# Attention block with a gated feed-forward layer on one core: batch 0's output projection and second norm in the last fourteen steps of the attention loop instead of its middle

## The chip, the cores and the metric

One Trainium2 chip, one of its cores, one launch. The metric is the device time of the whole kernel in microseconds (us), lower is better. The engines are TensorE (PE in the profile; PEld its weight loads), VectorE (DVE), ScalarE (ACT), GpSimd (POOL) and SyncE (SP, which here only issues DMAs). Each runs its own instructions in the order in which they are written, and they meet only in semaphores.

## The reference

For x of shape (2, 1024, 256), in float32:

```python
x = x + quaternion_layer(x)                  # one 256x256 product
h = tc_rmsnorm_1(x, cond)                    # g * x * rsqrt(mean(x*x) + eps) + b, g and b from cond
q, k, v = h @ Wq.T, h @ Wk.T, h @ Wv.T       # 16 heads of 16
o = softmax(q k.T / 4) @ v
x = x + o @ Wo.T
y = tc_rmsnorm_2(x, cond)
x = x + (silu(y @ gate_w.T) * (y @ hid_w.T)) @ out_w.T     # hidden size 1024
```

## The kernel before

Tokens are 16 tiles of 128, in four chunks of 512: chunks 0 and 1 are batch 0, chunks 2 and 3 batch 1. There are three stages. A **preparation** makes q, k and v. The **attention loop** has 128 steps (`NSTEP`): for each of 8 groups of 4 heads (four groups a batch) and each half of 512 queries, eight steps over the tiles of 128 keys. What stands **behind the loop** (the list `fin`) is the feed-forward layer, 32 units of which (`("F", n)`) make gate and hidden products and then the output product, and between its first units the rest of the attention's output work.

In a **narrow step** (0 to 113) TensorE computes four score tiles of 512 columns for the softmax (L1214), four for the row maxima of a later group (L1141, reduced by VectorE, L982), and the products with v (L1249); ScalarE takes the exponentials (L850). From step `WIDE` = 114 on there are no maxima left: in these fourteen **wide steps** TensorE issues four score matmuls (L1230), then what else is placed there, then the four products with v of the step before (L1249, 512 columns), and ScalarE takes two exponentials of 1024 columns (L843). VectorE has almost nothing to do there. PSUM has eight banks: in the wide steps six of them hold three pairs of score tiles, bank 7 the products with v, and bank 6 is the only one for everything else.

**Side items** are put among the steps. ("T", n) transposes row maxima, ("O", n) the attention output of eight steps; they come every eighth step. The other items, in the table `placed`, are the work that follows the attention:

- ("a_T", c, k): four transposes (L1097) of attention output of chunk c, then its split in a high and a low part (`at_hi`, `at_lo`);
- ("WO", c, pair): the output projection of two token tiles, twelve matmuls of 256 columns (L1123), to which x is added;
- then the squares of the new x, their mean (`ms`), its inverse root by a power on GpSimd (L587), the scaled tokens `xs2`, and `add_residuals` on GpSimd (`x1 += attn`, 1024 columns, L592);
- ("y_T", c, k): four transposes of `xs2`, then the norm's scale and shift into `yn_f` and the split into `yn_hi` and `yn_lo`, which the feed-forward units of chunk c read.

For batch 0 these items stand at steps 60 to 90 before the change, and ScalarE empties their PSUM banks (a copy, or the norm's scale and shift) while GpSimd makes the two parts, adds x and scales the tokens. For batch 1 they stand behind the loop, where ScalarE, VectorE and GpSimd share them. An item in the loop holds its bank until its reader has counted a semaphore (`e_used`). The order on each engine is the order of the code; nothing is scheduled.

Of the kernel before, what the change touches and what calls it, by code (L numbers as in the profile page):

```python
# [22 lines left out]
P = 128  # L23
BATCH, SEQ, D = 2, 1024, 256
# [6 lines left out]
CT = 4  # L31
# [33 lines left out]
def build(nc, xt, cond, coef, wt, gwt, ft, out):  # L65
# [4 lines left out]
    with ctx:  # L70
# [109 lines left out]
        def head_rows(e, n):  # L180
# [14 lines left out]
        square_steps = {half_done + 1: (0, 0), half_done + 4: (0, 1), half_done + 12: (1, 0), half_done + 15: (1, 1)}  # L195
        mean_steps = {half_done + 6: 0, half_done + 17: 1}


        cuts = [placed[step] for step in sorted(placed) if placed[step][0] != "WO"]
        cut_no = {item: i for i, item in enumerate(cuts)}  # L200

# [23 lines left out]
        for step in range(NSTEP):  # L225
            for item in ([("S", step, i) for i in (2, 3) if step < WIDE] + side_items(step)
                         + [("S", step + 1, i) for i in range(2) if step + 1 < WIDE]):
                e_no[item] = len(e_no)
        wide_sides = {item for step in range(WIDE, NSTEP) for item in side_items(step)}
# [45 lines left out]
        for key, (n, _, _) in plan.items():  # L275
            if key[0] in ("QK", "V"):
# [5 lines left out]
        fin = ([("F", 0), last_output, ("a_T", 2, 0), ("a_T", 2, 1), ("F", 1), ("WO", 2, 0), ("WO", 2, 1), ("F", 2),  # L282
                ("a_T", 3, 0), ("a_T", 3, 1), ("SC", 2), ("F", 3), ("WO", 3, 0), ("WO", 3, 1), ("F", 4),
                ("y_T", 2, 0), ("y_T", 2, 1), ("F", 5), ("SC", 3), ("F", 6), ("y_T", 3, 0), ("y_T", 3, 1)]
               + [("F", n) for n in range(7, len(ffn_units) + OUT_LAG)])
# [57 lines left out]
        wo_added = sem("wo_added")  # L343
# [5 lines left out]
        cut_hi_ready = sem("cut_hi_ready")  # L349
        cut_ready = sem("cut_ready")  # L350
# [31 lines left out]
        def e_bank(*item):  # L382
            return psum[:, 6 if item in wide_sides else 4 + e_no[item] % EB, :]
# [32 lines left out]
        def wait_e_used(eng, *item):  # L416

            if item in (("T", 0), last_output):
                wait_evacuated(eng, *item)
            else:  # L420
                eng.wait_ge(e_used, e_no[item] + 1)
# [12 lines left out]

        def wait_cut(eng, *item):

            eng.wait_ge(cut_ready, cut_no[item] + 1)

        def cut_dst(item, part):
            hi_lo = (at_hi, at_lo) if item[0] == "a_T" else (yn_hi[item[1]], yn_lo[item[1]])  # L440
            return hi_lo[part][:, item[2], :]
# [116 lines left out]
        def _(pool):  # L558
# [35 lines left out]
            def low_part2(c, kt):  # L594
                pool.wait_ge(yn_hi_ready, KT * (c - BCH) + kt + 1)
                nc.gpsimd.tensor_tensor(yn_lo[c][:, kt, :], yn_f[:, kt, :], yn_hi[c][:, kt, :].bitcast(f32),
                                        ALU.subtract).then_inc(yn_lo_ready, 1)
# [41 lines left out]
            for step in range(NSTEP):  # L639
# [7 lines left out]
                for item in side_items(step):  # L647
                    if item[0] == "O":
                        normalise(item[1])
                    elif item[0] == "T":  # L650
                        split_maxima(item[1])
                    elif item[0] == "WO":
                        wait_e_used(pool, *item)
                        t = item[1] * CT + 2 * item[2]
                        nc.gpsimd.tensor_tensor(attn[:, t:t + 2, :], attn[:, t:t + 2, :], x1[:, t:t + 2, :], ALU.add
                                                ).then_inc(wo_added, 1)
                if step in mean_steps:
                    c = mean_steps[step]
                    pool.wait_ge(squares_done, NT + CT * (c + 1))
                    nc.gpsimd.tensor_scalar(ms[:, 1, c * CT:(c + 1) * CT], sumsq[:, 1, c * CT:(c + 1) * CT],  # L660
                                            1.0 / D, NEPS, ALU.mult, ALU.add).then_inc(ms_ready, 1)
                    inverse_root(1, c)
                    pool.wait_ge(inv_ready, NCH + c + 1)
                    t = slice(c * CT, (c + 1) * CT)

                    if c:
                        wait_e_used(pool, "y_T", c - 1, 1)
                    nc.gpsimd.tensor_tensor(xs2[:, :, :], attn[:, t, :],
                                            inv_rms[:, 1, t].unsqueeze(2).to_broadcast([P, CT, D]), ALU.mult
                                            ).then_inc(ys_ready, 1)  # L670
                    pool.wait_ge(ys_ready, c + 1)
                    add_residuals(c)
                    pool.wait_ge(x12_ready, c + 1)
                item = placed.get(step)
                if item in cut_no:
                    n = cut_no[item]
                    wait_e_used(pool, *item)
                    nc.gpsimd.tensor_copy(cut_dst(item, 0), yn_f[:, n % 2, :]).then_inc(cut_hi_ready, 1)
                    pool.wait_ge(cut_hi_ready, n + 1)
                    nc.gpsimd.tensor_tensor(cut_dst(item, 1), yn_f[:, n % 2, :], cut_dst(item, 0).bitcast(f32),  # L680
                                            ALU.subtract).then_inc(cut_ready, 1)
# [20 lines left out]
        def _(act):  # L702
# [16 lines left out]
            def norm_affine(norm, c, kt):  # L719
# [3 lines left out]
                if norm and c == BCH:  # L723
                    act.wait_ge(cut_ready, len(cuts))
                elif norm:
                    act.wait_ge(yn_lo_ready, KT * (c - BCH - 1) + kt + 1)
                elif c:
                    act.wait_ge(xn_lo_ready, KT * (c - 1) + kt + 1)
# [82 lines left out]
            def side_item(item):  # L811

                act.wait_ge(scores_filled, e_no[item] + 1)
                src = e_bank(*item)
                if item[0] == "T":
                    ins = copy_maxima(item[1], src)
                elif item[0] == "O":
                    ins = copy_outputs(item[1], src)
                elif item[0] == "WO":
                    t = item[1] * CT + 2 * item[2]  # L820
                    ins = nc.scalar.activation(attn[:, t:t + 2, :], src.rearrange("p (t d) -> p t d", t=2), ACT.Copy)
                else:
                    i = cut_no[item]
                    if i >= 2:
                        wait_cut(act, *cuts[i - 2])
                    if item[0] == "y_T":
                        ins = nc.scalar.activation(yn_f[:, i % 2, :], src, ACT.Identity,
                                                   scale=gb_col(item[1] // BCH, 1, 0, item[2]),
                                                   bias=gb_col(item[1] // BCH, 1, 1, item[2]))
                    else:  # L830
                        ins = nc.scalar.activation(yn_f[:, i % 2, :], src, ACT.Copy)
                ins.then_inc(e_used, 1)
# [3 lines left out]
            for s in range(NSTEP + 1):  # L836
# [15 lines left out]
                if s and s % LT == 0:  # L852
                    o = s // LT - 1
                    act.wait_ge(pv_done, s)
                    if o:
                        act.wait_ge(scores_filled, e_no["O", o - 1] + 1)
                    nc.scalar.activation(ot[:, :], O_BANK, ACT.Copy).then_inc(o_copied, 1)  # L857
                for item in side_items(s) if s < NSTEP else []:
                    side_item(item)

                if s in square_steps:
                    c, pair = square_steps[s]
                    act.wait_ge(wo_added, 2 * c + pair + 1)
                    for i in range(2):
                        sum_squares(1, c * CT + 2 * pair + i, attn[:, c * CT + 2 * pair + i, :])
# [41 lines left out]
        def _(dve):  # L907
# [76 lines left out]

            def reciprocal_sums(n):
# [52 lines left out]
            for s in range(NSTEP):  # L1038
# [4 lines left out]
                if s % LT == 2 and s > LT and len(max_items(s)) < 2:  # L1043
                    reciprocal_sums(s // LT - 1)

            for step in fin:
# [17 lines left out]
                if what == "SC":  # L1064
                    c = rest[0]
                    dve.wait_ge(squares_done, NT + CT * (c + 1))
                    mean_squares(1, c)
                    scale_tokens(1, c, attn, xs2, ys_ready)
# [24 lines left out]
        def _(pe):  # L1093
# [92 lines left out]
            def do_side(item):  # L1186

                what, n = item[0], item[1]
                pe.wait_ge(e_used, e_no[item] - (0 if item in wide_sides else EB - 1))
# [7 lines left out]
                elif what == "WO":  # L1197
                    wait_cut(pe, "a_T", n, 1)
# [4 lines left out]
                last.then_inc(scores_filled, 1)  # L1203
# [14 lines left out]
            def wide_scores(s, pair):  # L1218
# [3 lines left out]
                elif n == 2:  # L1222
                    pe.wait_ge(e_used, e_no["T", NG * NHALF - 1])
# [112 lines left out]
            pe.wait_ge(wide_used, wide_no(NSTEP, 0))  # L1336
            for step in fin:
# [24 lines left out]
                if n < len(ffn_units):  # L1362
                    c, ht = ffn_units[n]
                    if n == 0:
                        pe.wait_ge(cut_ready, len(cuts))
                        pe.wait_ge(fw_ready, len(fw_steps))
                    if ht == 0 and c >= BCH:
                        pe.wait_ge(yn_lo_ready, KT * (c - BCH + 1))
# [72 lines left out]
```

## Time and profile before

| what | value |
|---|---|
| time, median of 3 runs | 574.06 us (570.61 to 580.15) |
| the profiled execution's own time | 572.87 us |
| its span, first to last instruction | 571.1 us |
| mean granted TensorE clock | 0.991 of full |
| preparation ends, narrow steps begin | about 86 us |
| wide steps begin | about 394 us |
| loop ends, feed-forward begins | about 424 us |

The span is 1.8 us less than the time, which lies around it. Busy shares are averages over the three stages, which have different limits, so the stages are read one by one: the narrow steps in stretches of eight, the wide steps instruction by instruction.

### The profile page before, as it was taken

What the parts mean: (1) busy time and instruction counts of PE and PEld (TensorE: products, weight loads), DVE (VectorE), ACT (ScalarE), POOL (GpSimd) and SP (SyncE); (2) the same over time, 40 slices, a digit from 0 to 9 for tenths busy, and PEclk for the clock granted to TensorE, in tenths of its full rate; (3) what the DMA queues carried; (4) which work ended last, traced back from release to release, by engine and by line L of the source; (5) the groups of instructions that cost most, each with busy time, mean ns of one, the idle gap of its engine ahead of it and who ended that gap; (6) DMA issues with size and microseconds to landing.
All of it is one profiled execution on the core that took longest, in us unless ns stands there. A gap on an engine that the chain in (4) does not pass through costs nothing.

```text
span 571.1 us, 10548 instructions
## 1 busy us (share of the span) xinstructions
PE 550.7 (96%) x4272; PEld 308.6 (54%) x4272; DVE 381.6 (67%) x407; ACT 379.3 (66%) x734; POOL 157.6 (28%) x171
## 2 busy tenths in 40 slices
PE   8979999999999999999999999998999999999997
PEld 7765663333333333344343333333248988888886
DVE  5946878999999999988878989996004442121211
ACT  3643437888888888888879988988984432222322
POOL 5302430230231230031622620000005543233232
PEclk9997998999999999999999999999999999999999
DMA  5494984117017016006005100000000001010001
GB/s 215 148 310 166 248 254 137 34 40 146 7 41 151 1 50 104 1 3 114 2 5 92 22 5 1 3 3 3 1 1 1 1 0 39 1 37 1 27 12 38
DMA packets 15669, 35.21 MB, mean 62 GB/s; under 512 B 1900, under 2 KB 4588, under 8 KB 15620
## 3 DMA queue, kind: packets, MB, share of 16 engines
q1 hardware_dynamic: 13764, 27.98, 18.8%
q10 hardware_dynamic: 1856, 6.55, 4.0%
q8 instruction: 34, 0.56, 0.4%
q14 instruction: 15, 0.12, 0.1%
HBM read 19.48 MB, written 14.94 MB: 60 GB/s over the span
## 4 chain that ended last, share of the span: by engine, by line
PE 85%; ACT 6%; DVE 3%; issue 2%; DMA 2%; SPq 1%; POOL 0%; DVEq 0%; ACTq 0%
PE psum L1123 31%; PE psum L1141 26%; PE psum L1249 22%; PE psum L1097 3%; ACT prob L843 2%; ACT prob L850 2%; ACT ot L857 2%; DVE nmax L982 1%; DMA q_st<-scr_qk 1%; PE psum L1214 1%; PE psum L1230 1%; PE psum L1267 1%; PE psum L1173 1%; DMA qc<-in_coef 1%; DVE xs L971 0%
## 5 line engine op out<-in xcount | busy, mean ns | idle before, releaser
L982 DVE TENSOR_REDUCE nmax<-psum 128x1 f32<-128x1024 f32 x256 | 310.4, 1222 | 41.7 <-PE psum L1141 41.6
L850 ACT ACTIVATE prob<-psum 128x512 f32<-128x512 f32 x456 | 247.3, 597 | 37.1 <-PE psum L1214 18.5
L1141 PE MATMUL psum<-k_st,q_st 48*128 48x512 f32 x512 | 184.7, 451 | 5.1 <-DMA q_st<-scr_qk 4.5
L1214 PE MATMUL psum<-q_st,k_st 50*128 50x512 f32 x456 | 167.9, 447 | 0.5 <-ACT prob L850 0.3
L1249 PE MATMUL psum<-prob,v_sb 128*17 128x256 f32 (+1 forms) x1928 | 158.2, 400 | 6.4 <-ACT ot L857 4.3
L1141 PEld LDWEIGHTS psum<-k_st,q_st 48*128 48x128 f32 x512 | 75.9, 187 | 108.7 <-DVE nmax L982 60.9
L1081 DVE TENSOR_TENSOR h_f<-psum,silu_g 128x512 f32<-128x512 f32 x32 | 22.1, 691 | 101.0 <-PE psum L1123 94.5
L1249 PEld LDWEIGHTS psum<-prob,v_sb 128*17 128x17 f32 x1928 | 32.4, 95 | 85.6 <-ACT prob L850 61.5
L900 ACT ACTIVATE silu_g<-psum 128x512 f32<-128x512 f32 x32 | 19.1, 597 | 78.7 <-PE psum L1123 78.6
L1214 PEld LDWEIGHTS psum<-q_st,k_st 50*128 50x128 f32 x456 | 68.6, 185 | 3.7 <-ACT prob L850 2.3
L697 POOL TENSOR_TENSOR h_lo<-h_f,h_hi 128x512 fp32r<-128x512 f32 x32 | 41.6, 1299 | 71.0 <-ACT h_hi L876 71.0
L633 POOL TENSOR_TENSOR attn<-o_raw,rsum 128x256 f32<-128x256 f32 x16 | 10.0, 623 | 182.1 <-DVE rsum L990 182.1
L1123 PE MATMUL psum<-yn_hi,fw_lo 128*128 128x512 f32 x128 | 50.7, 396 | 0.0
L1123 PE MATMUL psum<-yn_lo,fw_hi 128*128 128x512 f32 x128 | 50.2, 392 | 0.0
L1123 PE MATMUL psum<-yn_hi,fw_hi 128*128 128x512 f32 x128 | 49.9, 390 | 0.0
L1123 PE MATMUL psum<-fo_hi,h_lo 128*128 128x256 f32 x128 | 36.2, 283 | 0.0
L1123 PE MATMUL psum<-fo_hi,h_hi 128*128 128x256 f32 x128 | 36.2, 283 | 0.0
L1123 PE MATMUL psum<-fo_lo,h_hi 128*128 128x256 f32 x128 | 36.2, 283 | 0.0
L843 ACT ACTIVATE prob<-psum 128x1024 f32<-128x1024 f32 x28 | 26.3, 1079 | 2.1 <-PE psum L1230 1.9
L1123 PEld LDWEIGHTS psum<-yn_hi,fw_hi 128*128 128x128 f32 x128 | 24.0, 188 | 5.3
L1123 PEld LDWEIGHTS psum<-yn_hi,fw_lo 128*128 128x128 f32 x128 | 24.1, 189 | 5.0 <-issue 0.8
L1123 PEld LDWEIGHTS psum<-yn_lo,fw_hi 128*128 128x128 f32 x128 | 24.2, 189 | 3.9
(118 smaller groups left out, 589.1 us busy)
## 6 DMA issues: line engine op xcount, KB each, us to landing
scr_qk<-qk_parts SPq DMA_DIRECT2D x16, 512.0 KB, 4.5
k_st<-scr_qk SPq DMA_DIRECT2D x12, 384.0 KB, 8.8
q_st<-scr_qk SPq DMA_DIRECT2D x12, 384.0 KB, 10.4
scr_qk<-qk_parts SPq DMA_DIRECT2D x16, 256.0 KB, 5.5
f_raw<-in_ft ACTq DMA_DIRECT2D x6, 512.0 KB, 3.8
x_t<-in_xt SPq DMA_DIRECT2D x3, 512.0 KB, 3.4
out_x<-attn SPq DMA_DIRECT2D x3, 512.0 KB, 3.4
k_st<-scr_qk ACTq DMA_DIRECT2D x2, 384.0 KB, 5.1
```

Of the source, the lines that this page charges most:

```text
L697: nc.gpsimd.tensor_tensor(h_lo[n % 3][:, :], h_f[n % 2][:, :], h_hi[n % 3][:, :].bitcast(f32), ALU.subtract).then_inc(h_lo_ready, 1)
L843: nc.scalar.activation(prob[:, first:first + 2, :], wide_slot(s, pair), ACT.Exp).then_inc(wide_used, 1)
L850: nc.scalar.activation(prob_of(s, *HEAD_ORDER[h]), e_bank("S", s, h), ACT.Exp).then_inc(e_used, 1)
L857: nc.scalar.activation(ot[:, :], O_BANK, ACT.Copy).then_inc(o_copied, 1)
L900: nc.scalar.activation(silu_g[n % 2][:, :], bank_of("gate", n), ACT.Silu).then_inc(free_sem("gate", n), 1)
L982: nc.vector.tensor_reduce(out=nmax[:, b, e, pair, t:t + 1], in_=slot, axis=AX.XY, op=ALU.max, negate=True).then_inc(max_used, 1)
L1081: nc.vector.tensor_tensor(h_f[n % 2][:, :], bank_of("hid", n), silu_g[n % 2][:, :], ALU.mult).then_inc(free_sem("hid", n), 1)
L1097: last = nc.tensor.transpose(dst[:, i * P:(i + 1) * P], src, ident[:, :])
L1123: ins = nc.tensor.matmul(dst, s, m, start=first and i == 0, stop=last and i == len(passes) - 1)
L1141: return nc.tensor.matmul(max_slot(item)[:, half, :], q_st[g % SLOTS][rows, pair, lt * P:(lt + 1) * P], k_st[g % SLOTS][rows, pair, half * ...
L1214: nc.tensor.matmul(e_bank("S", s, i), k_st[g % SLOTS][rows, pair, kt * P:(kt + 1) * P], q_st[g % SLOTS][rows, pair, half * HALF:(half + 1) ...
L1249: last = nc.tensor.matmul(O_BANK[32 * h:32 * h + VW, cols], v_sb[:, b * LT + kt, hg * GH + h, :], prob_of(s, e, pair)[:, cols], start=kt = ...
```

## The change

The table `placed` is written anew: batch 0's items go to steps 115 to 125. ("y_T", 1, 0) and ("y_T", 1, 1) go into `fin`, right behind the first feed-forward unit, and what stood there moves back by one unit. Items in the wide steps get a pair of semaphores of their own (`side_filled`, `side_used`). ScalarE and GpSimd lose batch 0's items; a new function of VectorE, `placed_item`, splits a_T, adds x to WO, takes the squares (`tensor_tensor_reduce`), the mean and, for chunk 0, the scaled tokens right behind ("WO", 0, 1), and does the norm's scale and shift and the high part of y_T. GpSimd keeps the inverse root, `add_residuals` and the low part of y_T, at the items' new places. Each new item takes bank 6, so TensorE starts it only when the one before has been emptied.

```diff
-        half_done = NSTEP // BATCH
-        placed = {half_done + d: item for d, item in (
-            (-4, ("a_T", 0, 0)), (-3, ("a_T", 0, 1)), (-1, ("WO", 0, 0)), (2, ("WO", 0, 1)),
-            (5, ("a_T", 1, 0)), (7, ("a_T", 1, 1)), (10, ("WO", 1, 0)), (13, ("WO", 1, 1)),
-            (15, ("y_T", 0, 0)), (18, ("y_T", 0, 1)), (23, ("y_T", 1, 0)), (26, ("y_T", 1, 1)))}
+        placed = {WIDE + 1: ("a_T", 0, 0), WIDE + 2: ("a_T", 0, 1), WIDE + 3: ("WO", 0, 0), WIDE + 4: ("WO", 0, 1),
+                  WIDE + 5: ("a_T", 1, 0), WIDE + 6: ("a_T", 1, 1), WIDE + 8: ("WO", 1, 0), WIDE + 9: ("WO", 1, 1),
+                  WIDE + 10: ("y_T", 0, 0), WIDE + 11: ("y_T", 0, 1)}
...
-        fin = ([("F", 0), last_output, ("a_T", 2, 0), ("a_T", 2, 1), ("F", 1), ("WO", 2, 0), ("WO", 2, 1), ("F", 2),
...
+        fin = ([("F", 0), last_output, ("y_T", 1, 0), ("y_T", 1, 1), ("F", 1), ("a_T", 2, 0), ("a_T", 2, 1),
+                ("F", 2), ("WO", 2, 0), ("WO", 2, 1), ("F", 3), ("a_T", 3, 0), ("a_T", 3, 1), ("SC", 2),
...
+                    elif item[0] == "WO" and item[2] == 1:
                         wait_e_used(pool, *item)
...
+                        inverse_root(1, item[1])
+                        add_residuals(item[1])
+                    elif item[0] == "y_T":
+                        low_part2(item[1], item[2])
...
+            def placed_item(item):
+
+                what, c, i = item
+                src = e_bank(*item)
+                dve.wait_ge(side_filled, side_no[item] + 1)
+                if what == "a_T":
+                    link(nc.vector.tensor_copy(at_hi[:, i, :], src))
+                    nc.vector.tensor_tensor(at_lo[:, i, :], src, at_hi[:, i, :].bitcast(f32), ALU.subtract
+                                            ).then_inc(side_used, 1)
+                elif what == "WO":
+                    t = c * CT + 2 * i
+                    nc.vector.tensor_tensor(attn[:, t:t + 2, :], src.rearrange("p (t d) -> p t d", t=2),
+                                            x1[:, t:t + 2, :], ALU.add).then_inc(side_used, 1)
+                    if i == 1:
+                        dve.wait_ge(side_used, side_no[item] + 1)
+                        for k in range(c * CT, (c + 1) * CT):
+                            dve.wait_ge(squares_done, NT + max(k - 1, 0))
+                            nc.vector.tensor_tensor_reduce(out=squares[:, k % 2, :], in0=attn[:, k, :], in1=attn[:, k, :],
+                                                           scale=1.0, scalar=0.0, op0=ALU.mult, op1=ALU.add,
+                                                           accum_out=sumsq[:, 1, k:k + 1]).then_inc(squares_done, 1)
+                        dve.wait_ge(squares_done, NT + CT * (c + 1))
+                        mean_squares(1, c)
+                        if c == 0:
+                            scale_tokens(1, c, attn, xs2, ys_ready)
+                else:
+                    nc.vector.tensor_scalar(yn_f[:, i, :], src, gb_col(c // BCH, 1, 0, i), gb_col(c // BCH, 1, 1, i),
+                                            ALU.mult, ALU.add).then_inc(side_used, 1)
+                    dve.wait_ge(side_used, side_no[item] + 1)
+                    nc.vector.tensor_copy(yn_hi[c][:, i, :], yn_f[:, i, :]).then_inc(yn_hi_ready, 1)
+                    if item == wide_sides[-1]:
+                        scale_tokens(1, c + 1, attn, xs2, ys_ready)
...
             def do_side(item):
 
                 what, n = item[0], item[1]
-                pe.wait_ge(e_used, e_no[item] - (0 if item in wide_sides else EB - 1))
+                if item not in side_no:
+                    pe.wait_ge(e_used, e_no[item] - EB + 1)
+                elif side_no[item]:
+                    pe.wait_ge(side_used, side_no[item])
```

On **TensorE**, step 119 of the loop between the products with v of two steps. Before, it holds only scores (L1230) and products with v (L1249):

```order
L1249 MATMUL psum<-prob,v_sb 17x512 [waits wide_used]
L1249 MATMUL psum<-prob,v_sb 17x512 x3
L1230 MATMUL psum<-q_st,k_st 128x512 [waits wide_used]
L1230 MATMUL psum<-q_st,k_st 128x512
L1230 MATMUL psum<-q_st,k_st 128x512 [waits wide_used]
L1230 MATMUL psum<-q_st,k_st 128x512
L1249 MATMUL psum<-prob,v_sb 17x512 [waits wide_used]
L1249 MATMUL psum<-prob,v_sb 17x512 x3
```

Now, from the item of step 119 to the end of step 120 (scores are L1215, products with v L1234):

```order
L1077 MATMUL psum<-ident,attn 128x128 [waits o_normed,side_used]
L1077 MATMUL psum<-ident,attn 128x128 x3
L1234 MATMUL psum<-prob,v_sb 17x512 [waits wide_used]
L1234 MATMUL psum<-prob,v_sb 17x512 x3
L1215 MATMUL psum<-q_st,k_st 128x512 [waits max_loaded3,wide_used]
L1215 MATMUL psum<-q_st,k_st 128x512
L1215 MATMUL psum<-q_st,k_st 128x512 [waits wide_used]
L1215 MATMUL psum<-q_st,k_st 128x512
L1077 MATMUL psum<-ident,attn 128x128 [waits o_normed,side_used]
L1077 MATMUL psum<-ident,attn 128x128 x3
L1234 MATMUL psum<-prob,v_sb 17x512 [waits wide_used]
L1234 MATMUL psum<-prob,v_sb 17x512 x3
```

The two groups of transposes are ("a_T", 1, 0) and ("a_T", 1, 1); the second waits for `side_used` of the first, and step 119's products with v are queued behind it.

On **VectorE**, the end of the loop. Before, the last maxima, two reciprocals, and then the work behind the loop:

```order
L990 RECIPROCAL rsum<-o_raw 128x16 [waits o_normed,e_used]
L982 TENSOR_REDUCE nmax<-psum 128x1 [waits max_filled] x15
L990 RECIPROCAL rsum<-o_raw 128x16 [waits o_normed,e_used] x2
L1081 TENSOR_TENSOR h_f<-psum,silu_g 128x512 [waits tile_filled,evacuated4]
L990 RECIPROCAL rsum<-o_raw 128x16 [waits o_normed,evacuated6]
```

Now, from the last of chunk 0's four squares (each an instruction and a read of its accumulator) on:

```order
L947 ISA squares,sumsq<-attn 128x256 [waits squares_done]
L947 ISA sumsq 128x1
L908 TENSOR_SCALAR ms<-sumsq 128x4 [waits squares_done]
L916 TENSOR_SCALAR xs<-attn,inv_rms 128x256 [waits inv_ready]
L916 TENSOR_SCALAR xs<-attn,inv_rms 128x256 x3
L936 CAST at_hi<-psum 128x512 [waits side_filled]
L937 TENSOR_TENSOR at_lo<-psum,at_hi 128x512 [waits vector_step]
L936 CAST at_hi<-psum 128x512 [waits side_filled]
L937 TENSOR_TENSOR at_lo<-psum,at_hi 128x512 [waits vector_step]
L967 RECIPROCAL rsum<-o_raw 128x16 [waits o_normed,side_used]
```

Squares, mean and scaled tokens of chunk 0 stand ahead of the instructions that empty ("a_T", 1, 0).

On **GpSimd**, the same stretch. Before, two splits of maxima, then the first instruction behind the loop:

```order
L633 TENSOR_TENSOR attn<-o_raw,rsum 128x4x64 [waits rsum_ready]
L604 CAST nmax_t<-nmax_raw 16x128 [waits nmax_saved,e_used]
L606 TENSOR_TENSOR nmax_t<-nmax_raw,nmax_t 16x128 [waits nmax_hi_ready]
L633 TENSOR_TENSOR attn<-o_raw,rsum 128x4x64 [waits rsum_ready] x2
L697 TENSOR_TENSOR h_lo<-h_f,h_hi 128x512 [waits h_hi_ready]
```

Now:

```order
L592 TENSOR_TENSOR nmax_t<-nmax_raw,nmax_t 16x128 [waits nmax_hi_ready]
L573 TENSOR_TENSOR inv_rms<-ms,neg_half 128x4 [waits ms_ready,side_used]
L578 TENSOR_TENSOR x<-x,attn 128x1024
L619 TENSOR_TENSOR attn<-o_raw,rsum 128x4x64 [waits rsum_ready]
L573 TENSOR_TENSOR inv_rms<-ms,neg_half 128x4 [waits ms_ready,side_used]
L578 TENSOR_TENSOR x<-x,attn 128x1024
L582 TENSOR_TENSOR yn_lo<-yn_f,yn_hi 128x512 [waits yn_hi_ready] x2
L619 TENSOR_TENSOR attn<-o_raw,rsum 128x4x64 [waits rsum_ready]
```

Each residual addition (L578) follows its inverse root (L573) without a wait of its own; the low parts of chunk 0's y follow the second.

## Rows read from the trace of the kernel before

**Rows 1.** The page: the chain that ended last, by engine

```profile
PE 85%; ACT 6%; DVE 3%; issue 2%; DMA 2%; SPq 1%; POOL 0%; DVEq 0%; ACTq 0%
```

**Rows 2.** Busy time by stretch of eight steps: PE, PEld, DVE, ACT, POOL, PEclk, DMA

```profile
234.00:257.47 23.47, 23.16 (x217) 9.79 (x218) 19.54 (x18) 19.75 (x39) 6.42 (x8) 1.00 0.01 2
257.47:281.34 23.87, 23.54 (x218) 9.96 (x218) 19.73 (x18) 20.90 (x47) 10.72 (x12) 1.00 0.39 69
281.34:306.54 25.20, 24.76 (x225) 10.99 (x226) 19.72 (x18) 21.18 (x47) 7.00 (x8) 1.00 0.01 3
306.54:328.44 21.90, 21.59 (x206) 8.36 (x207) 19.69 (x18) 19.52 (x38) 10.56 (x11) 1.00 0.43 75
328.44:349.72 21.28, 20.97 (x202) 7.91 (x202) 19.69 (x18) 18.85 (x37) 3.19 (x5) 1.00 0.01 3
349.72:370.43 20.71, 20.40 (x198) 7.49 (x199) 19.54 (x18) 18.19 (x36) 1.35 (x3) 1.00 0.01 3
```

**Rows 3.** The chain, middle of the loop: start us, us, what

```profile
243.41 0.59 PE psum L1097 x4
...
251.90 1.60 PE psum L1123 x12
```

**Rows 4.** Timeline of PE, wide steps: start us, us, instruction [idle before it]

```profile
396.18 1.05 PE L1249 MATMUL psum<-prob,v_sb 128*17 128x512 f32 x8
397.16 0.73 PE L1230 MATMUL psum<-q_st,k_st 50*128 50x512 f32 x4
397.83 1.05 PE L1249 MATMUL psum<-prob,v_sb 128*17 128x512 f32 x8
...
409.47 0.63 PE L1097 MATMUL psum<-ident,ot 128*128 128x128 f32 x4 [0.70 <-ACT ot L857]
```

**Rows 5.** Timeline of ACT: exponentials of the wide steps, an accumulator read behind them

```profile
397.73 11.11 ACT L843 ACTIVATE prob<-psum 128x1024 f32<-128x1024 f32 x12 [0.46 <-PE psum L1230]
...
433.35 0.19 ACT L710 ACTIVATION_READ_ACCUMULATOR squares<-attn 128x1 f32 x1
```

**Rows 6.** Groups of instructions: count | busy us, mean ns | idle before

```profile
L592 POOL TENSOR_TENSOR x<-x,attn 128x1024 f32<-128x1024 f32 x4 | 9.5, 2387 | 6.6 <-DVE attn L1061 6.4
...
L587 POOL TENSOR_TENSOR inv_rms<-ms,neg_half 128x4 f32<-128x4 f32 x8 | 8.1, 1013 | 26.2 <-DVE ms L963 26.0
...
L1061 DVE TENSOR_TENSOR attn<-psum,x 128x512 f32<-128x512 f32 x4 | 2.8, 691 | 2.2 <-PE psum L1123 2.1
...
L963 DVE TENSOR_SCALAR ms<-sumsq 128x4 f32<-128x4 f32 x6 | 1.3, 220 | 0.0
```

**Rows 7.** Timeline of DVE: scaled tokens twice, and four additions

```profile
13.78 1.14 DVE L971 TENSOR_SCALAR xs<-x,inv_rms 128x256 f32<-128x256 f32 x4 [1.23 <-POOL inv_rms L587]
...
441.45 2.17 DVE L971 TENSOR_SCALAR xs<-attn,inv_rms 128x256 f32<-128x256 f32 x4 [1.13 <-POOL inv_rms L587]
...
567.01 1.43 DVE L1088 TENSOR_TENSOR attn<-psum,x 128x256 f32<-128x256 f32 x4 [2.82 <-PE psum L1123]
```

**Rows 8.** Timeline of POOL beside the second row above

```profile
441.39 1.30 POOL L697 TENSOR_TENSOR h_lo<-h_f,h_hi 128x512 fp32r<-128x512 f32 x1
```

**Rows 9.** Timeline of PE in the preparation: its longest wait

```profile
44.22 1.42 PE L1141 MATMUL psum<-k_st,q_st 48*128 48x512 f32 x4 [4.47 <-DMA q_st<-scr_qk]
```

**Rows 10.** Busy time and PEclk in short stretches; columns as in Rows 2

```profile
40.00:44.00 4.00, 0.00 (x0) 0.00 (x0) 1.19 (x3) 2.08 (x8) 1.01 (x1) 0.95 1.02 242
44.00:46.00 2.00, 1.78 (x5) 1.16 (x6) 0.56 (x1) 0.25 (x1) 0.00 (x0) 0.50 0.17 29
...
50.00:52.00 2.00, 2.00 (x8) 1.25 (x7) 2.00 (x2) 0.35 (x1) 0.98 (x1) 0.90 0.74 289
...
88.00:90.00 2.00, 2.00 (x14) 0.66 (x12) 1.68 (x2) 1.16 (x3) 0.00 (x0) 0.50 0.92 309
```

**Rows 11.** Timeline of PE behind the loop: two groups of transposes, what follows

```profile
427.05 1.04 PE L1097 MATMUL psum<-ident,attn 128*128 128x128 f32 x8
427.85 0.48 PE L1123 MATMUL psum<-yn_hi,fw_lo 128*128 128x512 f32 x1
```

More of the change, by code:

```diff
@@ L225, in build @@
         for step in range(NSTEP):
-            for item in ([("S", step, i) for i in (2, 3) if step < WIDE] + side_items(step)
+            for item in ([("S", step, i) for i in (2, 3) if step < WIDE] + (side_items(step) if step < WIDE else [])
                          + [("S", step + 1, i) for i in range(2) if step + 1 < WIDE]):
                 e_no[item] = len(e_no)
-        wide_sides = {item for step in range(WIDE, NSTEP) for item in side_items(step)}
+        wide_sides = [item for step in range(WIDE, NSTEP) for item in side_items(step)]
+        side_no = {item: i for i, item in enumerate(wide_sides)}
         maxima_first = 2
@@ L281, in build @@
         ffn_units = [(c, ht) for c in range(NCH) for ht in range(HT)]
-        fin = ([("F", 0), last_output, ("a_T", 2, 0), ("a_T", 2, 1), ("F", 1), ("WO", 2, 0), ("WO", 2, 1), ("F", 2),
-                ("a_T", 3, 0), ("a_T", 3, 1), ("SC", 2), ("F", 3), ("WO", 3, 0), ("WO", 3, 1), ("F", 4),
-                ("y_T", 2, 0), ("y_T", 2, 1), ("F", 5), ("SC", 3), ("F", 6), ("y_T", 3, 0), ("y_T", 3, 1)]
-               + [("F", n) for n in range(7, len(ffn_units) + OUT_LAG)])
+        fin = ([("F", 0), last_output, ("y_T", 1, 0), ("y_T", 1, 1), ("F", 1), ("a_T", 2, 0), ("a_T", 2, 1),
[3 rows of a table added]
+               + [("F", n) for n in range(8, len(ffn_units) + OUT_LAG)])
         ring[0] = 0
@@ L382, in e_bank @@
         def e_bank(*item):
-            return psum[:, 6 if item in wide_sides else 4 + e_no[item] % EB, :]
+            return psum[:, 6 if item in side_no else 4 + e_no[item] % EB, :]
         def wide_no(s, pair):
@@ L433, in fw_dst @@
             return (fo_hi, fo_lo)[part][:, ht:ht + 2, :].rearrange("p a d -> p (a d)")
[L435 to L441, printed above, removed]
         def wait_saved(eng, n):
@@ L722, in norm_affine @@
                 act.wait_ge(gb_ready, 1)
[L723 to L726, printed above, removed]
+                if norm:
+                    act.wait_ge(yn_lo_ready, KT * (c - 1) + kt + 1)
                 elif c:
@@ L811, in side_item @@
             def side_item(item):
-                act.wait_ge(scores_filled, e_no[item] + 1)
+                if item in side_no:
+                    act.wait_ge(side_filled, side_no[item] + 1)
+                else:
+                    act.wait_ge(scores_filled, e_no[item] + 1)
                 src = e_bank(*item)
[L815 to L832, printed above, removed]
+                ins = copy_maxima(item[1], src) if item[0] == "T" else copy_outputs(item[1], src)
+                ins.then_inc(side_used if item in side_no else e_used, 1)
             act.wait_ge(w_lo_ready, 4)
@@ L858, in _ @@
                 for item in side_items(s) if s < NSTEP else []:
[L859 to L865, printed above, removed]
+                    if item[0] in ("T", "O"):
+                        side_item(item)
                 if s in fw_loads:
@@ L1042, in _ @@
                     item_of_max_slot(item)
-                if s % LT == 2 and s > LT and len(max_items(s)) < 2:
+                if s % LT == 2 and s > LT and s >= WIDE:
                     reciprocal_sums(s // LT - 1)
+                if s in placed:
+                    placed_item(placed[s])
             for step in fin:
@@ L1067, in _ @@
                     mean_squares(1, c)
+                    wait_filled(dve, "y_T", c - 1, 1)
                     scale_tokens(1, c, attn, xs2, ys_ready)
@@ L1188, in do_side @@
                 what, n = item[0], item[1]
-                pe.wait_ge(e_used, e_no[item] - (0 if item in wide_sides else EB - 1))
+                if item not in side_no:
+                    pe.wait_ge(e_used, e_no[item] - EB + 1)
+                elif side_no[item]:
+                    pe.wait_ge(side_used, side_no[item])
+                else:
+                    pe.wait_ge(e_used, len(e_no))
                 dst = e_bank(*item)
@@ L1197, in do_side @@
                 elif what == "WO":
-                    wait_cut(pe, "a_T", n, 1)
+                    wait_e_used(pe, "a_T", n, 1)
                     last = project_out(dst, item[2])
@@ L1202, in do_side @@
                     last = blocks(dst, y_blocks(item[2]))
-                last.then_inc(scores_filled, 1)
+                last.then_inc(side_filled if item in side_no else scores_filled, 1)
             def scores(s, i):
@@ L1336, in _ @@
             pe.wait_ge(wide_used, wide_no(NSTEP, 0))
+            pe.wait_ge(side_used, len(side_no))
             for step in fin:
@@ L1364, in _ @@
                     if n == 0:
-                        pe.wait_ge(cut_ready, len(cuts))
                         pe.wait_ge(fw_ready, len(fw_steps))
-                    if ht == 0 and c >= BCH:
-                        pe.wait_ge(yn_lo_ready, KT * (c - BCH + 1))
+                    if ht == 0:
+                        pe.wait_ge(yn_lo_ready, KT * (c + 1))
                     cols = slice(ht * P, (ht + 1) * P)
```

48 lines of the change are left out of this document (10 added, 38 removed), and 2 rows, old and new, of the table fin.

## The prediction

> **What bounds the kernel now.** I read the chain that ended last first: TensorE holds 85% of it [rows 1], so time is won or lost only where TensorE's own work changes or where it is made to wait. The shares by stage come next. In the narrow steps a stretch of eight takes 20.71 us, of which TensorE is busy 20.40, VectorE 19.54 and ScalarE 18.19, in its last row [rows 2]: TensorE sets the pace, the two others are close behind. The reader should see that the five stretches that hold batch 0's items take more than that: 23.47, 23.87, 25.20, 21.90 and 21.28 us [rows 2].
>
> The wide steps differ. TensorE's work in one is 0.98 us of products with v (396.18 to 397.16) and 0.67 of scores (397.16 to 397.83), 1.65 in all [rows 4], while ScalarE needs 11.11 us for twelve exponentials, 1.85 a step [rows 5]. So ScalarE sets the pace there, VectorE is idle, and TensorE has 0.20 us a step to spare: for fourteen steps 2.8 us. That is all the free room that TensorE's moved work finds; the items themselves need far more.
>
> **What is removed from the middle.** The surplus over 20.71 of the five stretches is 2.76 + 3.16 + 4.49 + 1.19 + 0.57 = 12.17 us. It can be checked from the items: four transposes cost the chain 0.59 us and a projection of twelve matmuls 1.60 [rows 3]; eight of the first and four of the second make 4.72 + 6.40 = 11.12, and the last 1.05 are waits, most of them in the third stretch, where ScalarE is busy 21.18 us against 18.19. All of this goes, and nothing is late in its place: the stretch at 349.72 is what such steps are without items. **-12.2 us.**
>
> **What is added in the wide steps, TensorE's work.** A step with four transposes takes 1.65 + 0.59 = 2.24 us instead of 1.85, one with a projection 1.65 + 1.60 = 3.25. Six of the first and four of the second (two y_T items leave the loop) add 6 x 0.39 + 4 x 1.40 = 7.9. TensorE also idles 0.70 us where ScalarE empties bank 7 (before 409.47) [rows 4]; some 0.2 of that is absorbed. **+7.7 us**, between 7.2 (all of that wait absorbed) and 7.9. ScalarE's exponentials are hidden in the steps with items.
>
> **What is added as a wait.** Bank 6 is the only one for items, and VectorE empties it in the order of its code. Most items pass: a_T needs two VectorE instructions on a 512-column bank, 0.69 each [rows 6] and some 0.1 between, 1.5 us, and TensorE comes back for the bank after 0.98 + 0.67 = 1.65. The exception is ("a_T", 1, 0) in step 119. I count from the last matmul of ("WO", 0, 1). VectorE then has in its queue:
> - the addition of x, 0.69 [rows 6], 0.75 with its hand-over;
> - four squares of 256 columns. No row shows this instruction. The nearest is the addition of 256 columns, four in 1.43 us [rows 7], but each square also reads an accumulator, which on ScalarE costs 0.19 [rows 5]. I take 0.5 each, 2.0; bounds 1.4 (the reads hidden) and 2.6 (0.65 each, nothing overlapped);
> - the mean, 0.22 [rows 6], 0.3 with its wait;
> - GpSimd's inverse root, 1.01 [rows 6], 1.1 with both hand-overs;
> - four scaled tokens. Undisturbed they take 1.14, but 2.17 when GpSimd had begun a 1.30 us subtraction 0.06 us before them [rows 7, 8]. Here GpSimd begins, right behind the inverse root and without a wait, `add_residuals`, which lasts 2.39 [rows 6]. If the first token waits for its end, the four take about 2.3 + 1.1 = 3.4. Bounds 1.14 and 3.4; I take 3.4, because GpSimd's next instruction began first at 441.39 too;
> - then a_T's own two instructions, 1.5.
>
> Sum: 0.75 + 2.0 + 0.3 + 1.1 + 3.4 + 1.5 = 9.05 us. In the same time TensorE has products 0.98, scores 0.67, the transposes 0.59, products 0.98 and scores 0.67, 3.89 us, and then stands before ("a_T", 1, 1), whose semaphore is a_T(1,0)'s. Behind it are queued the products with v of step 119, and behind these bank 7's emptying; ScalarE runs dry after two exponentials. **+5.1 us**, bounds 9.05 - 0.6 - 2.26 - 3.89 = 2.3 and 5.7.
>
> The Trainium skill (SBUF — State Buffer, "Who interferes with whom") states that VectorE and GpSimd share one pair of SBUF ports under an exclusive lock: whichever begins first holds it for its whole instruction and the other blocks. By that rule the four tokens cost the 3.4 taken above; if the 1.03 us of rows 7 were a fixed loss instead, they would cost 2.17 and the sum below would be 1.2 us lower.
>
> **The later items.** ("WO", 1, 1) in step 123 is followed by the same squares, but not by scaled tokens: VectorE is free after 0.75 + 2.0 + 0.3 = 3.05 us, ("y_T", 0, 0) leaves its bank at 3.75, and TensorE wants it at 3.89. No wait, with 0.14 us in hand; with squares of 0.65 it is 0.5 us. The first feed-forward unit now needs y's low parts from GpSimd, which has the root, 2.39 of residuals and two low parts of 1.3 (rows 8's kind) to do after step 123's mean: 3.1 + 1.1 + 2.4 + 2.6, and up to 1 us of collisions, 9.2 to 10.2 us after ("WO", 1, 1). TensorE needs 0.98 + 2.24 + 2.24 for the rest of step 123 and for 124 and 125, 3.7 for 126 and 127, and 1.65 or so to drain, 10.8. Covered, by 0.6 us at the least. Chunk 1's tokens are wanted only after that unit.
>
> **What the wait does to TensorE's clock.** Its longest idle stretch now is 4.47 us, before 44.22 [rows 9]. The granted clock was at full until its last moments (0.95 over 40 to 44), then at half, 0.50, from 44 to past 50 [rows 10]: some 6.2 us at 1.2 instead of 2.4 GHz. It was also 0.50 over 88 to 90, where the narrow steps begin, so for 2 us or more. In the middle of the loop nothing idles it that long. A wait of 5.1 us is longer than the one that cost the clock. Work done at half clock takes twice as long, so 2 to 6.2 us at half cost 1.0 to 3.1, and the steps behind the wait (121 to 123) are TensorE's own. I take a value nearer to the idle stretch's, since that is the same kind of gap: **+2.4 us.**
>
> **Behind the loop.** Two y_T items more: two such groups took from 427.05 to 427.85 [rows 11]. **+0.8 us.** The order of the units and of batch 1's items relative to each other stays, so their own waits stay.
>
> **Sum.** -12.2 + 7.7 + 5.1 + 2.4 + 0.8 = +3.8 us on the profiled execution's 572.87: **576.7**. That execution lies 1.2 under the median of the runs shown, whose spread (570.61 to 580.15) is larger than the change.
>
> **Rivals.**
> - *The wait comes, the clock holds*: without the clock's term 574.3. For it: one case of a 4.5 us gap is thin evidence, and bounds of the wait reach down to 2.3.
> - *VectorE is quick*: tokens not blocked, squares at 0.36, a wait of 2.3 or less, clock at full: 572.87 - 12.2 + 7.7 + 2.3 + 0.8 = 571.5. Were the wait nil, 569.2: faster than before. Against it: GpSimd's start ahead of VectorE in rows 7 and 8.
> - *A second queue*: squares of over 0.65 us. Then ("y_T", 0, 0) holds bank 6 for 0.5 us or more, and GpSimd's low parts arrive after TensorE has drained, so the first feed-forward unit waits: 0.5 + 1 to 3 us on top, a wait of 5.7, the clock at 3.1. 572.87 - 12.2 + 7.9 + 5.7 + 3.1 + 0.8 + 1.5 to 3.5 = 579.7 to 581.7, slower than before, the point being 0.6 us of cover ahead of ("F", 0).
> - *The change does nothing*: excluded, the items' places on TensorE differ in the program.
>
> **How the numbers follow.** Chances: forecast 0.45, wait with full clock 0.27, quick VectorE 0.17, second queue 0.09, something else 0.02. The forecast is the likeliest, so 576.7. With the bounds of its terms (wait -1.2, with the tokens at 2.17, to +0.6; clock -1.4 to +0.7; work -0.5 to +0.2) it spans 573.6 to 578.2. Taking in the two lower rivals and the noise of a median of runs that scatter by some us gives 569.5 to 581. No case comes near 2% of the time, 11.5 us, which is about what a measurement of this kernel can tell from no change: even the whole of the middle's 12.2 us would be needed for that, and the same work returns. Faster by over 2% 0.01, slower 0.03, within 0.96.
>
> **What would show it.** In the changed kernel's trace: eight-step stretches of 20.7 us between 234 and 382; the wide steps some 12.2 us earlier and 12.8 longer (15.2 with the clock); on TensorE one wait of about 5 us in step 120, released by VectorE's `at_lo`; before it four scaled tokens taking some 3.4 us beside GpSimd's residuals; a granted clock of half behind it. A wait under 3 us or a clock at full proves those terms wrong; a wait ahead of the first feed-forward unit shows the second queue.

## The result, and the profile after

The changed kernel takes 575.41 us (median of 20 runs) against 572.1 us (20 runs of the kernel before on the same chips): a ratio of 1.0053, 95% interval 1.003 to 1.0075, so some 3 us slower, clear of the measurement's own scatter and far inside 2%. Some executions of any kernel here are some 9 us longer at a lower mean clock; they count in the medians but in no ratio and no count of runs below, and as the profiles of E2 and E5 are of such executions, only single instructions and short stretches are read from them. The forecast was +3.8 us and 576.7.

The middle of the loop first, in stretches of eight steps of the kernel after (columns as in Rows 2). They answer to those of [rows 2]:

```profile
236.76:257.47 20.71, 20.39 (x198) 7.50 (x199) 19.54 (x18) 18.19 (x36) 1.35 (x3) 1.00 0.01 2
257.47:278.18 20.71, 20.40 (x199) 7.50 (x201) 19.54 (x18) 18.19 (x36) 1.36 (x3) 1.00 0.48 79
278.18:298.88 20.70, 20.39 (x197) 7.48 (x198) 19.52 (x18) 18.17 (x36) 1.36 (x3) 1.00 0.01 3
298.88:319.59 20.71, 20.40 (x198) 7.50 (x198) 19.54 (x18) 18.18 (x36) 1.36 (x3) 1.00 0.45 79
319.59:340.30 20.71, 20.40 (x198) 7.50 (x199) 19.54 (x18) 18.18 (x36) 1.35 (x3) 1.00 0.01 3
...
384.35:429.16 44.81, 38.29 (x256) 15.78 (x255) 22.28 (x45) 28.09 (x31) 11.38 (x10) 0.92 0.01 2
```

All stretches are at 20.70 or 20.71, so the 12.17 us of the middle are gone whole. The last row is the wide steps, from the first wide scores to the end of the last products with v. The same stretch of the kernel before:

```profile
393.78:423.72 29.94, 26.08 (x183) 6.79 (x183) 1.64 (x3) 27.02 (x31) 1.98 (x4) 1.00 0.01 2
```

It has grown by 14.9 us, and the mean clock in it has fallen from 1.00 to 0.92. Most of that is TensorE's own work for the items, 7.7 (E1, below); the rest is one wait and two spells of half clock. Step 120 on TensorE shows where (timeline of PE, the idle time before an instruction in brackets):

```profile
400.87 0.66 PE L1077 MATMUL psum<-ident,attn 128*128 128x128 f32 x4
401.46 1.05 PE L1234 MATMUL psum<-prob,v_sb 128*17 128x512 f32 x8
402.44 0.73 PE L1215 MATMUL psum<-q_st,k_st 50*128 50x512 f32 x4
407.51 1.12 PE L1077 MATMUL psum<-ident,attn 128*128 128x128 f32 x4 [4.34 <-DVE at_lo L937]
408.56 1.91 PE L1234 MATMUL psum<-prob,v_sb 128*17 128x512 f32 x8
410.40 0.74 PE L1215 MATMUL psum<-q_st,k_st 50*128 50x512 f32 x4
```

TensorE stands 4.34 us ahead of ("a_T", 1, 1), until VectorE's `at_lo` of ("a_T", 1, 0). Behind the wait the transposes last 1.12 and the products 1.91 us, where those at 400.87 and 401.46 lasted 0.66 and 1.05: the granted clock was 0.51 over 407 to 409, so half. What VectorE and GpSimd did meanwhile stands in the chain that ended last (start, us, what):

```profile
399.33 0.70 DVE attn L941
...
400.06 0.42 DVE squares L947
...
401.56 0.18 DVE ms L908
...
401.88 1.02 POOL inv_rms L573
402.89 0.03 issue
402.92 3.21 DVE xs L916 x4
406.13 0.61 DVE at_hi L936
406.74 0.02 issue
406.76 0.70 DVE at_lo L937
```

and on GpSimd, in its timeline:

```profile
401.88 1.01 POOL L573 TENSOR_TENSOR inv_rms<-ms,neg_half 128x4 f32<-128x4 f32 x1 [13.14 <-DVE ms L908]
402.85 2.34 POOL L578 TENSOR_TENSOR x<-x,attn 128x1024 f32<-128x1024 f32 x1
```

The residual addition began at 402.85, the first scaled token at 402.92; the four took 3.21 us where [rows 7] has 1.14 with nothing beside them. The queue is the one that the prediction wrote out, piece by piece.

### The profile page after: what moved, and what is told of

Its sections match the earlier page's. It is cut to its first block, busy times and chain, and to the rows that moved or that the text cites. A ratio compares the mean times of both kernels' runs of the same rounds, so it can differ in the third digit from the quotient of the medians.

```text
span 577.5 us, 10543 instructions
## 1 busy us (share of the span) xinstructions
PE 554.0 (96%) x4272; PEld 309.8 (54%) x4272; DVE 403.4 (70%) x451; ACT 372.5 (64%) x708; POOL 138.1 (24%) x151
## 4 chain that ended last, share of the span: by engine, by line
PE 86%; DVE 5%; ACT 4%; DMA 2%; issue 2%; SPq 1%; POOL 0%; DVEq 0%; ACTq 0%; POOLq 0%
PE psum L1103 30%; PE psum L1121 26%; PE psum L1234 23%; PE psum L1077 3%; ACT ot L806 2%; ACT prob L797 2%; DMA q_st<-scr_qk 1%; DVE nmax L927 1%; PE psum L1215 1%; DVE xs L916 1%; PE psum L1199 1%; PE psum L1252 1%; PE psum L1153 1%; DMA qc<-in_coef 1%; DVE xn_lo L997 0%
## 5 line engine op out<-in xcount | busy, mean ns | idle before, releaser
L1234 PE MATMUL psum<-prob,v_sb 128*17 128x256 f32 (+1 forms) x1928 | 160.5, 405 | 5.3 <-ACT ot L806 4.3
L1234 PEld LDWEIGHTS psum<-prob,v_sb 128*17 128x17 f32 x1928 | 32.5, 95 | 85.2 <-ACT prob L797 68.2
```

The lines of the kernel that those rows point to most:

```text
L1234: last = nc.tensor.matmul(O_BANK[32 * h:32 * h + VW, cols], v_sb[:, b * LT + kt, hg * GH + h, :], prob_of(s, e, pair)[:, cols], start=kt = ...
```

## The experiments

Six kernels. E1 and E2 each take one piece of the wait out of the changed kernel, E3 and E5 fill the wait with work, E4 is the move without the change of engines, and E6, built on E1, measures the term of TensorE's work. Differences between two of them are taken from their ratios to the kernel before; by the intervals each is uncertain by 1.7 to 2.5 us.

### E1: the scaled tokens later

```diff
                         mean_squares(1, c)
-                        if c == 0:
-                            scale_tokens(1, c, attn, xs2, ys_ready)
...
+                    if (c, i) == (1, 1):
+                        scale_tokens(1, 0, attn, xs2, ys_ready)
```

The second piece stands behind `at_lo` in the branch of a_T.

> The changed kernel, with chunk 0's scaled tokens taken out of VectorE's queue behind the second projection and put behind ('a_T', 1, 1); nothing is left out. Theory (VectorE's queue ahead of a_T(1,0) holds bank 6, and TensorE waits 4.4 us for it in step 120): the tokens are 3.2 us of that queue and the hand-over to GpSimd 1.2, so the wait goes, and the half clock behind it too: 4.4 + 1.3 to 1.5 = 5.7 to 5.9 us less than the changed kernel's 575.4, so 569.6, which is 2.5 us under before. Rival (the wait is ScalarE's or the loop's in disguise, and comes back in later steps): 574 to 575.4. In the trace: no idle time of TensorE over 0.5 us in step 120, granted clock at full from 390 us on by the theory.

Measured: 569.24 us, ratio 0.9948 (0.9923 to 0.9973): 6.0 us under the changed kernel and 3 under the kernel before. VectorE's timeline at the place:

```profile
396.30 0.17 DVE L908 TENSOR_SCALAR ms<-sumsq 128x4 f32<-128x4 f32 x1
396.38 0.68 DVE L936 CAST at_hi<-psum 128x512 fp32r<-128x512 f32 x1
397.10 0.69 DVE L937 TENSOR_TENSOR at_lo<-psum,at_hi 128x512 fp32r<-128x512 f32 x1
398.54 0.69 DVE L936 CAST at_hi<-psum 128x512 fp32r<-128x512 f32 x1 [0.75 <-PE psum L1077]
399.27 0.69 DVE L937 TENSOR_TENSOR at_lo<-psum,at_hi 128x512 fp32r<-128x512 f32 x1
399.88 1.13 DVE L916 TENSOR_SCALAR xs<-attn,inv_rms 128x256 f32<-128x256 f32 x4
```

a_T(1,0) now comes right behind the mean. On TensorE, from the list of its waits in the wide steps, only this is left:

```profile
PE psum L1215 <- DVE nmax L927: 1.1, 1, 1.1
PE psum L1234 <- ACT prob L790: 1.0, 2, 0.8
PE psum L1077 <- ACT ot L806: 0.2, 1, 0.2
```

Two of these three the kernel before has as well (1.08 before 395.54, 0.78 before 422.74); the third was 0.70 there [rows 4]. The wait does not come back in a later step. The wide steps, read on TensorE as before, last 37.62 us (380.58 to 418.20), 7.68 more than in the kernel before, with the clock at full. The rival of a wait in disguise falls.

### E2: GpSimd's residual addition later

```diff
                     if item[0] == "O":
                         normalise(item[1])
+                        if step >= WIDE:
+                            add_residuals(0)
...
                         inverse_root(1, item[1])
-                        add_residuals(item[1])
+                        if item[1]:
+                            add_residuals(item[1])
```

> The changed kernel, with GpSimd's add_residuals of chunk 0 moved from right behind the inverse root to step 121; VectorE's order is unchanged, nothing is left out. Theory (the first scaled token waits for the whole of GpSimd's 2.34 us addition): the four tokens take 1.15 instead of 3.21 us and the wait in step 120 falls from 4.4 to 2.3 us: 2.1 us less, 573.3, and 1.3 less again (572.0) if so short a wait leaves the clock at full. Rival (a token loses a fixed time, or the four are slow because they read what was just written): tokens at 2.2 to 3.2 us, wait 3.4 to 4.4, time 574.4 to 575.4.

Measured: 572.09 us, ratio 0.9993 (0.9966 to 1.002), 3.4 us under the changed kernel. VectorE's timeline, and TensorE's list of waits:

```profile
407.97 1.14 DVE L919 TENSOR_SCALAR xs<-attn,inv_rms 128x256 f32<-128x256 f32 x4 [1.19 <-POOL inv_rms L573]
```

```profile
PE psum L1080 <- DVE at_lo L940: 2.3, 1, 2.3
PE psum L1218 <- DVE nmax L930: 1.1, 1, 1.1
```

Nothing was changed on VectorE, and its four tokens fall from 3.21 to 1.14 us, the wait from 4.3 to 2.3. So 2.07 us of the wait were GpSimd's addition, and the loss is not a fixed one: it was 1.03 beside a subtraction of 1.30 us and 2.07 beside an addition of 2.34, each time what was left of GpSimd's instruction when the first token began, less 0.2. Not every VectorE instruction loses: in E1 the `at_hi` and `at_lo` at 398.54 and 399.27, which read PSUM, took their usual 0.69 us each while GpSimd's addition ran from 397.59 to 399.97.

This is how the exclusive lock on the shared pair of ports would act that the Trainium skill states (SBUF — State Buffer, "Who interferes with whom"); the runs agree, with the 1.03 and 2.07 us above.

Of the 3.4 us that the kernel gained, 2.07 are the wait's. Whether the clock gave the rest is open: in the profiled execution it was at full (1.00) behind the 2.3 us wait, but only 2 of E2's 10 runs have a mean clock of 0.993 or more, and the difference lies within the uncertainty.

### E3 and E5: the wait filled with matmuls

```diff
+                        if s == WIDE + 6:
+                            repeat_scores(s + 1, FILL)
                         for item in side_items(s):
                             do_side(item)
```

`repeat_scores` computes the pair of score tiles that comes next anyway, FILL times more, into the free pair of banks: FILL is 10 in E3 and 17 in E5.

> The changed kernel, with extra work for TensorE: ahead of ('a_T', 1, 1) in step 120 it computes the first score pair of step 121 ten times more, about 3.35 us of matmuls inside the 4.4 us that it waits there. Nothing is left out. Theory (the idle stretch halves the clock behind it, and costs 1.3 us there beside the wait itself): the granted clock stays at full from 390 to 420 us, the transposes and products behind the wait take 0.59 and 0.98 instead of 1.05 and 1.84, and the time falls by 1.3 us to 574.1. Rival (the slow instructions behind the wait are not the idle time's doing): time the same, 575.4, or up to 3 us more if the extra matmuls delay the next items.

Measured: 573.63 us, ratio 1.0016 (0.9991 to 1.0042), 2.1 us under the changed kernel. But ten repeats took only 2.46 us where 3.35 had been expected, 2.10 stayed idle, and in the profiled execution the clock fell all the same:

```profile
400.00 2.46 PE L1226 MATMUL psum<-q_st,k_st 50*128 50x512 f32 x20
404.56 0.79 PE L1078 MATMUL psum<-ident,attn 128*128 128x128 f32 x4 [2.10 <-DVE at_lo L938]
405.28 1.91 PE L1245 MATMUL psum<-prob,v_sb 128*17 128x512 f32 x8
```

That row spoke for the rival, the time against it, so the fill was made longer.

> As the filled wait before, with seventeen repeats of the score pair instead of ten: in the first try they took 0.246 us each, so seventeen take 4.2 of the 4.4 us that TensorE waits in step 120, where ten left 2.1 us idle and the clock still fell behind them in the profiled run. Nothing is left out. Theory (the idle stretch, not the wait's place, halves the clock): no idle time over 0.5 us in step 120, granted clock at full over 400 to 412 us, the most frequent mean clock of the runs is 0.994 as in before and not 0.991 as in the changed kernel, and the time is 575.4 - 1.3 to 1.5 = 574.0, no better than with ten by more than 0.5 us. Rival (the clock falls there in any case, for instance because of the score pairs): clock half behind it and time as the changed kernel's.

Measured: 572.77 us, ratio 1.0019 (0.9999 to 1.0039), 1.9 us under the changed kernel and, as expected, no better than E3. TensorE's timeline:

```profile
408.04 4.05 PE L1226 MATMUL psum<-q_st,k_st 50*128 50x512 f32 x34
412.60 0.66 PE L1078 MATMUL psum<-ident,attn 128*128 128x128 f32 x4 [0.51 <-DVE at_lo L938]
413.18 1.05 PE L1245 MATMUL psum<-prob,v_sb 128*17 128x512 f32 x8
```

With 34 matmuls more in the same place the kernel is faster: what stands behind them takes 0.66 and 1.05 us instead of 1.12 and 1.91, at a granted clock of 1.00 over 410 to 420. The mean granted clock of the single runs says the same. Of the changed kernel's 17 runs none is above 0.991; of E5's 10, eight are at 0.993 or above, and of E3's 11, six, so that ten repeats often held the clock too; of the kernel before, 10 of the 15 runs beside E5 are. At 0.991 the changed kernel's five runs have a median of 574.1 us, at 0.994 E5's six have 572.6, which puts the clock's share at some 1.5 us; the kernel before differs by 1.3 (573.3 and 572.0) between the same two values. The rival falls.

### E4: the move alone

```diff
-        placed = {half_done + d: item for d, item in (
...
+        placed = {WIDE + d: item for d, item in (
+            (1, ("a_T", 0, 0)), (2, ("a_T", 0, 1)), (3, ("WO", 0, 0)), (4, ("WO", 0, 1)),
+            (5, ("a_T", 1, 0)), (6, ("a_T", 1, 1)), (8, ("WO", 1, 0)), (9, ("WO", 1, 1)),
+            (10, ("y_T", 0, 0)), (11, ("y_T", 0, 1)), (12, ("y_T", 1, 0)), (13, ("y_T", 1, 1)))}
...
+        square_steps = {WIDE + 4: (0, 0), WIDE + 5: (0, 1), WIDE + 9: (1, 0), WIDE + 10: (1, 1)}
+        mean_steps = {WIDE + 6: 0, WIDE + 11: 1}
```

> The kernel before, with its twelve items of batch 0 moved to steps 115 to 127, but emptied by ScalarE and split by GpSimd as before (squares on ScalarE in steps 118, 119, 123, 124, means in 120 and 125). Nothing is left out. Theory (free room in the wide steps is TensorE's 0.20 us a step, and ScalarE has none): ScalarE gets 8.0 us of copies and 3.6 of squares on top of 27.2, so the steps cost more than in the changed kernel, and the last low parts come from GpSimd after the loop has drained, so that the first feed-forward unit waits 3 to 5 us: 576 to 581. Rival (who empties the banks does not matter, since TensorE's work sets the steps): 569 to 575.

Measured: 587.02 us, ratio 1.024 (1.0202 to 1.0277), 13.7 us over the kernel before. The side was right, the size was not (576 to 581 expected). TensorE's waits between 383.5 and 442 us:

```profile
PE psum L1123 <- POOL at_lo L680: 6.2, 2, 4.0
PE psum L1097 <- POOL xs L668: 3.2, 1, 3.2
PE psum L1123 <- issue: 2.1, 1, 2.1
PE psum L1097 <- ACT yn_f L831: 1.3, 1, 1.3
```

I had added up ScalarE's load and missed what waits in GpSimd's queue. Of the 6.2 us, 2.1 are ahead of chunk 0's first projection: each a_T goes through a copy on ScalarE and then 0.61 and 1.28 us on GpSimd. The other 4.0 are ahead of chunk 1's. There ScalarE's copy was done at 408.42, but GpSimd was busy with chunk 0's mean, inverse root, scaling and addition from 406.95 to 412.65 (its timeline):

```profile
408.33 1.89 POOL L668 TENSOR_TENSOR xs<-attn,inv_rms 128x1024 f32<-128x1024 f32 x1
410.30 2.35 POOL L592 TENSOR_TENSOR x<-x,attn 128x1024 f32<-128x1024 f32 x1
412.71 0.61 POOL L678 CAST at_hi<-yn_f 128x512 fp32r<-128x512 f32 x1
```

So it is the changed kernel's queue once more, on another engine. Chunk 1's tokens wait for GpSimd too (3.2), and so does the first feed-forward unit (the 2.1 under "issue": the last low part ends at 438.95, the unit begins at 439.16), where 3 to 5 had been expected. Behind each of the three waits of 2.1, 4.0 and 3.2 us the clock fell (0.58 over 394 to 396, 0.60 over 414 to 418, 0.73 over 430 to 434; a projection's twelve matmuls took 2.83 us instead of 1.60 twice), which by my estimate from these lengths costs some 4 of the 13.7 us and was not in the expectation. The move pays only together with VectorE's emptying, which is worth 1.024 / 1.0053, some 10.6 us. That emptying alone, at the old places, was not tried: in the narrow steps items and scores count the same semaphore in one order, which two emptying engines would break.

### E6: one pass of the projection

```diff
-                    last = project_out(dst, item[2])
+                    for i in range(2):
+                        t = slice((2 * item[2] + i) * P, (2 * item[2] + i + 1) * P)
+                        for kt in range(KT):
+                            last = nc.tensor.matmul(dst[:, i * D:(i + 1) * D], at_hi[:, kt, t], wo_hi[:, kt, :],
+                                                    start=kt == 0, stop=kt == KT - 1)
```

> The kernel with chunk 0's tokens later, with two of the three passes of batch 0's output projection left out (only the high parts are multiplied, four matmuls of 256 columns an item instead of twelve), so batch 0's result is less exact. Theory (TensorE's own work sets the wide steps that hold items, 3.25 us for one with a projection against ScalarE's 1.85): four items lose 8 x 0.117 = 0.94 us each, 3.7 us in all: 569.2 - 3.7 = 565.5. Rival (ScalarE's exponentials or the emptying of bank 6 set them): a saving of 1 us or less.

Against E1, on which it is built, only this differs. Measured: ratio 0.987 (0.9839 to 0.9901), its three counted runs between 563.9 and 565.0 us. Against E1 that is 4.5 us less for 3.7 expected. Two steps on TensorE's timeline:

```profile
389.58 0.71 PE L1187 MATMUL psum<-wo_hi,at_hi 128*128 128x256 f32 x4
390.22 1.05 PE L1238 MATMUL psum<-prob,v_sb 128*17 128x512 f32 x8
391.20 0.73 PE L1219 MATMUL psum<-q_st,k_st 50*128 50x512 f32 x4
391.87 0.73 PE L1187 MATMUL psum<-wo_hi,at_hi 128*128 128x256 f32 x4
```

From item to item 2.29 us, without a gap, where E1's timeline has 3.26 from the products at 390.70 to those at 393.96: 0.97 a step, all of what was left out. TensorE sets the steps that hold items, even at 2.3 us.

## Why the prediction was right

The sum was +3.8 us, the measured ratio gives +3.0 (1.7 to 4.3). The mechanism was the forecast one; two terms were too large. Term by term:

- **What is removed, -12.2.** Right: all stretches at 20.70 or 20.71.
- **TensorE's work in the wide steps, +7.7.** Right: E1, which has the work and no wait, shows +7.68, and E6 that this work sets the steps.
- **The wait, +5.1.** Right in place, in releaser and in every member of the chain; 4.34 measured, 0.8 too long. The squares, for which no row stood, came every 0.34 us with the read of the accumulator overlapped (1.5 for four, not 2.0), near the low bound of 1.4, and the tokens took 3.21 for 3.4.
- **The four tokens beside GpSimd's addition.** I took 3.4 us and not the 2.17 of a fixed loss: right, 3.21 measured, and 1.14 without the addition (E2).
- **The clock, +2.4.** Right in kind, too large. Behind the wait the transposes and the products lost 0.46 and 0.86 us, 1.3 in the trace; 1.5 by the runs of E5. I had priced it by the preparation's gap, with 6.2 us at half; here the clock was back at 410.4, 2.9 us after work resumed. Nor did work at half clock take twice as long: 1.7 to 1.9 times (scores 1.15 for 0.67, transposes 1.05 for 0.59, products 1.84 for 0.98, from start to start). That the clock would fall at all rested on a single gap in the preparation; it held here, and the section on the hardware shows that it need not in each execution.
- **Behind the loop, +0.8.** From the end of the wide steps to the end of the span: 577.5 - 429.16 = 148.3 against 571.1 - 423.72 = 147.4, some +1.0 before rounding.
- **The later items.** No wait: TensorE's list for 384 to 429.2 has none but the one of step 120 and two that were there before. GpSimd's two low parts ended at 424.31 + 2.76 = 427.1, TensorE's last products at 429.2, so 2.1 us of cover stood ahead of the first feed-forward unit, where 0.6 "at the least" was forecast: the squares were 0.5 quicker, and the collisions, for which up to 1 us had been set aside, cost GpSimd next to nothing (the two low parts took 2.76 for 2.6). The second queue did not form.

-12.2 + 7.7 + 4.3 + 1.5 + 1.0 = +2.3, within the interval of the measured +3.0. The two errors, 0.8 in the wait and 0.9 in the clock, lie on the same side, so the sum owes nothing to one error hiding another. The time alone would hardly have told the forecast from its first rival (+1.4 without the clock's term, just outside the interval); the trace and E5 do. The profiled execution shows more, 577.5 against 571.1 us: its clock fell once more, at the start of the wide steps (below), and its preparation and the first narrow steps ended later, the first O item at 113.80 instead of 111.03, with none of the changed code in them. So the wide steps began 9.4 us earlier (384.35 for 393.78), not 12.2. One execution's span was no measure of a 3 us effect; the 20 runs were.

## What to carry to other kernels

Moving work to where an engine idles is worth that idle time (here 0.2 us a step) and the waits that the work had in its old place (1.05 us), no more; what decides is the emptying engine's queue behind the one free bank. Before a late stage's work is put into an in-order queue, ask of each instruction whether anyone waits for what is queued behind it: the scaled tokens were wanted in step 124 and held up the bank wanted in step 120, and putting them two items back turned 3 us lost into 3 us won. And keep a long GpSimd instruction away from the moment at which VectorE begins a short one on the critical path.

## What the runs showed of the hardware

The granted clock falls behind less idling than I had thought, and not in every execution. In the profiles after and of E2, E3 and E5 it also fell at the start of the wide steps, behind a wait of 1.08 us; in those of the kernel before and of E1, E4 and E6 it did not, at the same wait. Short stretches of the kernel after (columns as in Rows 2):

```profile
384.00:386.00 2.00, 1.04 (x8) 0.52 (x4) 1.46 (x3) 1.10 (x2) 0.00 (x0) 1.00 0.00 0
386.00:388.00 2.00, 1.88 (x11) 0.43 (x11) 0.22 (x2) 1.27 (x3) 0.69 (x2) 0.64 0.00 0
388.00:390.00 2.00, 2.00 (x9) 0.64 (x6) 0.00 (x0) 0.43 (x1) 0.66 (x2) 0.51 0.04 8
```

There the products with v and the scores took 1.84 and 1.15 us instead of 0.98 and 0.67, 1.3 us lost. In step 120, 2.1 us of idling were enough in E3, and 2.3 in E2 were not. What tells such executions apart stays open. It is probably a good part of the runs' scatter, since each 0.003 of mean clock goes with 1 to 2 us, but no run shows that the scatter comes from these places. And 34 matmuls whose result nobody needed made a kernel some 1.9 us faster, by holding the clock.
